# A gated delta rule's recurrence laid out by batch, head and half of the value

## What is computed

```
q = silu(conv4(x Wq) + qcb); k = silu(conv4(x Wk) + kcb) / 8; v = silu(conv4(x Wv) + vcb)
a = sigmoid(x Wa + ba); beta = sigmoid(x Wb + bb)
for each token t:                       # S: 64 values x 64 keys, one for each batch and head
    err = S k_t - v_t
    S   = a_t * S - beta_t * err k_t^T  # a_t scales the rows (values) of S
    o_t = S q_t
o = layernorm over a head's 64 values of o, times ln_w, plus ln_b; o = o * sigmoid(x Wg); x = x + o Wo
```

## Time and profile before

| | us |
|---|---|
| median of three runs | 4137.81 (4136.82 to 4139.02) |
| profiled execution | 4136.74 |
| its span | 4134.7 |
| its setup and start, to the first turning of P | 117.2 |
| recurrence, from there to the last segment's end | to about 2570 |
| the other phases | the rest |

### The profile page before, as it was taken

The page is one execution under the profiler, slowest core; times in us unless marked ns, Lnnn a source line. Parts: engine busy times, 40 slices in busy tenths (PEclk is TensorE's granted clock), DMA queues, the critical chain, the costliest instruction groups (busy, mean ns, idle before and its releaser), DMA issues. The chain is left out here.

```text
span 4134.7 us, 113160 instructions
## 1 busy us (share of the span) xinstructions
PE 3272.3 (79%) x45929; PEld 2781.3 (67%) x45929; DVE 3376.5 (82%) x6184; ACT 2222.6 (54%) x5291; POOL 2340.3 (57%) x3045
## 2 busy tenths in 40 slices
PE   5777787777777777777777774378999979998998
PEld 4677777777777777777777774354666657755765
DVE  4899999999999999999999997216888868856884
ACT  4444444444444454444444442225888779937982
POOL 0667767767767767767767675332000058807860
PEclk9888888898898898888888896588999989998999
DMA  2110110111111111101101100410000011101110
GB/s 75 38 37 26 40 37 27 42 35 28 44 32 33 42 30 36 41 27 38 35 25 36 35 24 24 146 44 1 2 2 2 2 34 37 42 6 38 40 36 26
DMA packets 158097, 139.18 MB, mean 34 GB/s; under 512 B 67204, under 2 KB 110416, under 8 KB 157322
## 3 DMA queue, kind: packets, MB, share of 16 engines
q1 hardware_dynamic: 155274, 129.24, 11.3%
q0 software_dynamic: 2304, 2.71, 0.2%
HBM read 96.11 MB, written 16.82 MB: 27 GB/s over the span
## 5 line engine op out<-in xcount | busy, mean ns | idle before, releaser
L1102 DVE TENSOR_TENSOR a_tmp<-a_h,banks 128x128 f32<-128x128 f32 (+14 forms) x960 | 723.3, 753 | 82.4 <-POOL a_h L871 51.4
L1108 DVE TENSOR_REDUCE a_h<-a_tmp 128x64 f32<-128x128 f32 (+14 forms) x960 | 723.0, 753 | 26.4
L871 POOL TENSOR_TENSOR a_h<-a_h,a_a 128x128 f32<-128x128 f32 (+11 forms) x768 | 552.1, 719 | 174.0 <-DVE a_h L1108 162.8
L540 PE MATMUL banks<-a_xseg,a_w_k 128*128 128x128 f32 x2048 | 308.4, 325 | 138.3 <-DVE a_h L1108 134.4
L540 PEld LDWEIGHTS banks<-a_xseg,a_w_k 128*128 128x128 f32 x2048 | 302.4, 239 | 144.5 <-DVE a_h L1108 140.3
L540 PE MATMUL banks<-a_xseg,a_w_v 128*128 128x128 f32 x2048 | 299.2, 318 | 98.6 <-DVE a_h L1108 98.3
L540 PEld LDWEIGHTS banks<-a_xseg,a_w_v 128*128 128x128 f32 x2048 | 292.9, 233 | 103.8 <-DVE a_h L1108 103.3
L856 POOL TENSOR_TENSOR a_st<-a_st,a_ab 128x512 f32<-128x512 f32 x256 | 326.1, 1274 | 0.0
L613 PE MATMUL banks<-a_wm,a_kt 64*64 64x64 f32 x8192 | 257.2, 221 | 84.6 <-ACT a_wm L746 84.5
L613 PEld LDWEIGHTS banks<-a_wm,a_kt 64*64 64x64 f32 x8192 | 248.4, 137 | 95.8 <-ACT a_wm L746 94.1
L746 ACT ACTIVATE a_wm<-a_wt,k_ih_mask 128x256 f32<-128x256 f32 x512 | 211.4, 495 | 164.1 <-DVE a_wt L1122 164.1
(11 more groups left out here) (297 smaller groups left out, 8422.7 us busy)
## 6 DMA issues: line engine op xcount, KB each, us to landing
a_ab<-decays SPq DMA_DIRECT2D x512, 128.0 KB, 3.0
d_Vs<-d_V SPq DMA_DIRECT2D x128, 128.0 KB, 2.3
sent<-k_nothing SPq DMA_DIRECT2D x40, 64.5 KB, 2.3
b_xe<-sent SPq DMA_DIRECT2D x8, 322.5 KB, 3.2
a_xseg<-xn SPq DMA_DIRECT2D x32, 70.0 KB, 3.1
xn<-a_xnT SPq DMA_DIRECT2D x8, 256.0 KB, 2.8
decays<-a_dc SPq DMA_DIRECT2D x128, 8.0 KB
a_xrow<-in_L_attn_x SPq DMA_DIRECT2D x128, 16.0 KB
```

What stands on the lines that cost most here:

```text
L540: t = e.matmul(b[:, m * SW:(m + 1) * SW].rearrange("p (b t) -> p b t", b=NB), self.wT[n][:, j, ct * P:(ct + 1) * P], xs[:, :, off:off + SE ...
L871: e.tensor_tensor(self.history(ch, t + 1)[:, :, 0:t], self.history(ch, t)[:, :, 0:t], at, ALU.mult).then_inc(*self.s_hist.at((g, t)))
L1102: e.tensor_tensor(prod, both, gram, ALU.mult).then_inc(*step.at((g, t, "product")))
L1108: e.tensor_reduce(self.results(ch, t), prod, AX.X, ALU.add).then_inc(*step.at((g, t, "w")))
```

## The change

All of the recurrence gets another order of partitions: batch (4) x `par` (2) x head pair (8) x half of the values (2), instead of head pair and batch first. So a batch has 32 neighbouring partitions.

- U: the stationary matrix is K by time (32 rows of one batch), the moving one Wt as VectorE turned it; 32 rows hold the two halves' 16 tokens each, and the two halves of the values are neighbouring columns. No masked copy is made, `act_mask` goes. K is no longer doubled (`act_double` goes), its 1/8 moves into Kt's eviction, the Gram evictions and `beta8`.
- P: the stationary matrix is k and q of 16 tokens, interleaved (32 columns of one batch), the moving one the state; the result has tokens on the partitions. Both U and P do two batches in turn, two `par` each, and signal or wait per pair of batches.
- Values and gates (`pe_project_rows`): the stationary matrix is a batch's 32 tokens, the moving one 512 columns of weights, and the result has time on the partitions. The bias is a matmul of one row ahead of the others. One eviction takes 512 columns.
- Gram matrices: tokens of one batch on 32 partitions, two groups instead of four, each with buffers of its own (`Ga`, `Gb`) that one addition of GpSimd joins. Time rows of K: 32 matmuls of full depth instead of 64.
- The stepwise tiles that were by time and then value (a2, bv, P2, o2) are now by value and then time.
- Outputs: after VectorE has turned a segment, TensorE transposes it (`pe_turn`), and ScalarE scales it as it evicts (`act_affine`, 8 instructions of 128x128); the gating works on 128x512 blocks that lie as the projection of g leaves them.
- Setup makes beta by batch on the partitions at once; the transposes and copies go. The decays go to memory in one DMA instead of four.

```diff
-            self.kq = two("kq", [P, R, 3, SEG])
-            self.kraw, self.va = sb("kraw", [P, R, SEG]), sb("va", [P, SEG, R])
-            self.a2, self.bv, self.dc = two("a2_", [P, SEG, 32]), sb("bv", [P, SEG, 32]), two("dc", [P, SEG, 32])
+
+            self.kq = two("kq", [P, R, SEG, 2])
+
+            self.va = sb("va", [P, 32, 32])
+            self.a2, self.bv, self.dc = two("a2_", [P, 32, SEG]), sb("bv", [P, 32, SEG]), two("dc", [P, SEG, 32])
             self.dk = sb("dk", [P, CK, 32])
-            self.G1, self.G1b, self.g2 = sb("g1", [P, 2, CK, R]), sb("g1b", [P, 2, CK, 8]), sb("g2", [P, 2, CK, SEG])
-            self.Kt, self.ST = sb("kt", [P, R, DK]), sb("st", [P, R, DK])
-            self.Wt, self.Wm = sb("wt", [P, R, 32]), sb("wm", [P, R, 2, 32])
+            self.Ga, self.Gb = sb("ga", [P, 2, CK, H0]), sb("gb", [P, 2, CK, H0])
+            self.G1, self.g2 = sb("g1", [P, 2, CK, 32]), sb("g2", [P, 2, CK, SEG])
+
+            self.Kt, self.ST = sb("kt", [P, CH]), sb("st", [P, R, DK])
+            self.Wt = sb("wt", [P, 32, 32])
...
+    def pe_project_rows(self, e, q, n, s, half):
+
+        b = self.take(q, (n, s, half))
+        xs, part = self.xseg[s % 4], slice(half * BANK, half * BANK + BANK)
+        taps = TAPS if n in CONV else 1
+        e.matmul(b, self.c.ones_row[0:1, 0:P], self.bias_row[n][:, part], start=True, stop=False)
+        q.wait_ge(self.l_seg[s % 4], s)
+        for j in range(taps):
+            off = j if taps > 1 else PAD
+            for bi in range(NB):
+                t = e.matmul(b[bi * SEG:(bi + 1) * SEG, :], xs[:, bi, off:off + SEG], self.wT[n][:, j, part], start=False,
+                             stop=(j == taps - 1))
+        t.then_inc(*self.s_full.at((n, s, half)))
+
...
+    def pe_gram(self, e, q, s, par):
+        b = self.take(q, ("gram", s, par))
+        kq, ps = self.kq[s % 2], slice(par * DK, (par + 1) * DK)
+        q.wait_ge(self.s_evac, ("k", s, 1))
+        q.wait_ge(self.s_evac, ("q", s, 1))
+        for ct in range(NCT):
+            for bi in range(NB):
+                r = ct * NB + bi
+                t = e.matmul(b[bi * SEG:(bi + 1) * SEG, ct * 2 * SEG:(ct + 1) * 2 * SEG], kq[ps, r, :, 0],
+                             kq[ps, r].rearrange("p t z -> p (t z)"), start=True, stop=True)
+        t.then_inc(*self.s_full.at(("gram", s, par)))
...
+    def pe_turn(self, e, q, s, half):
+
+        b = self.take(q, ("turn", s, half))
+        q.wait_ge(self.s_turn, s)
+        for m in range(4):
+            i = 4 * (4 * half + m)
+            t = e.transpose(b[:, m * P:(m + 1) * P], self.o1[:, i:i + 4, :].rearrange("p i x -> p (i x)"), self.c.ident[:])
+        t.then_inc(*self.s_full.at(("turn", s, half)))
...
+        for pair in range(0, NB, 2):
             if g:
-                q.wait_ge(self.s_st, (g - 1, r // 8))
-            for par in range(2):
-                ps = slice(par * DK, (par + 1) * DK)
-                t = e.matmul(pb[ps, r * 2 * CK:(r + 1) * 2 * CK].rearrange("p (z t) -> p z t", z=2), self.ST[ps, r, :],
-                             kq[ps, r, 0:3:2, js], start=True, stop=True)
+                q.wait_ge(self.s_st, (g - 1, pair + 1))
+            for ct in range(NCT):
+                for bi in (pair, pair + 1):
+                    for par in range(2):
+                        ps, at = slice(par * DK, (par + 1) * DK), par * BANK + ct * DK
+                        t = e.matmul(pb[bi * SEG:(bi + 1) * SEG, at:at + DK], kq[ps, ct * NB + bi, js].rearrange("p t z -> p (t z)"),
+                                     self.ST[ps, bi * NCT + ct, :], start=True, stop=True)
         t.then_inc(*self.s_p.at(g))
...
-        q.wait_ge(self.s_evac, ("rows", s, 3))
-        for n in range(4):
-            q.wait_ge(self.s_wm, (g, n))
-            if n >= 2:
+        q.wait_ge(self.s_evac, ("rows", s, 1))
+        q.wait_ge(self.s_wt, g)
+        for pair in range(0, NB, 2):
+            if pair:
                 q.wait_ge(self.s_step, (g, "last", "q"))
             elif g:
-                q.wait_ge(self.s_st, (g - 1, n))
-            for m in range(8):
-                r = 8 * n + m
-                for par in range(2):
-                    ps = slice(par * DK, (par + 1) * DK)
-                    t = e.matmul(self.ubank(n)[ps, m * DK:(m + 1) * DK], self.Kt[ps, r, :],
-                                 self.Wm[ps, r].rearrange("p h i -> p (h i)"), start=True, stop=True)
-            t.then_inc(*self.s_u.at((g, n)))
+                q.wait_ge(self.s_st, (g - 1, 1))
+            for ct in range(NCT):
+                for bi in (pair, pair + 1):
+                    rows = slice(bi * SEG, (bi + 1) * SEG)
+                    for par in range(2):
+                        k0, x = ct * P + par * DK, 16 * par + 2 * ct
+                        t = e.matmul(self.ubank(bi)[par * DK:(par + 1) * DK, ct * DK:(ct + 1) * DK], self.Kt[rows, k0:k0 + DK],
+                                     self.Wt[rows, x:x + 2, :].rearrange("p h i -> p (h i)"), start=True, stop=True)
+            t.then_inc(*self.s_u.at((g, pair + 1)))
...
+    def act_project_rows(self, e, q, n, s, half):
+        q.wait_ge(self.s_full, (n, s, half))
+        if n == "v":
+            q.wait_ge(self.s_a2, s)
         elif s:
-            q.wait_ge(self.s_gadd, (s - 1, 3))
-        e.activation(oth, v[:, :, :, 0, :], ACT.Copy, scale=half_of[:, 0:1])
+            q.wait_ge(self.s_vt, s - 1)
+        e.activation(self.va[:, :, 16 * half:16 * half + 16].rearrange("p i x -> p x i"),
+                     self.held((n, s, half)).rearrange("p (x i) -> p x i", i=32),
+                     ACT.Sigmoid if n == "a" else ACT.Silu).then_inc(*self.s_evac.at((n, s, half)))
+
...
-    def act_mask(self, e, q, g):
-
-        q.wait_ge(self.s_wt, g)
-        for n in range(4):
-            rr = slice(8 * n, 8 * n + 8)
-            if g:
-                q.wait_ge(self.s_u, (g - 1, n))
-            for h in range(2):
-                t = e.activation(self.Wm[:, rr, h, :], self.Wt[:, rr, :], ACT.Copy, scale=self.cst["ih_mask"][:, h:h + 1])
-            t.then_inc(*self.s_wm.at((g, n)))
...
+    def act_affine(self, e, q, s, half):
+        key = ("turn", s, half)
+        q.wait_ge(self.s_full, key)
+        if s:
+            q.wait_ge(self.s_y, (s - 1, half))
+        for m in range(4):
+            ct = 4 * half + m
+            t = e.activation(self.oT[:, ct, :], self.held(key)[:, m * P:(m + 1) * P], ACT.Identity, scale=self.lnw[:, ct:ct + 1],
+                             bias=self.lnb[:, ct:ct + 1])
+        t.then_inc(*self.s_evac.at(key))
...
-            at = self.a2[s % 2][:, ch * CK + t, :].rearrange("p (i o) -> p i o", o=1).broadcast_to([P, 32, t])
+            at = self.a2[s % 2][:, :, ch * CK + t:ch * CK + t + 1].broadcast_to([P, 32, t])
...
-        e.tensor_reduce(self.tot[:], self.o2[s % 2][:], AX.X, ALU.add).then_inc(*self.s_tot.at(("mean", s)))
+        e.tensor_reduce(self.tot[:], self.o2[s % 2][:].rearrange("p i t -> p t i"), AX.X, ALU.add).then_inc(*self.s_tot.at(("mean", s)))
     def dve_spread(self, e, q, s):
         q.wait_ge(self.s_squared, s)
         q.wait_ge(self.s_full, ("mean", s))
-        e.tensor_reduce(self.tot[:], self.o1[:].rearrange("p (t x) i -> p t (x i)", x=1), AX.X,
-                        ALU.add).then_inc(*self.s_tot.at(("dev", s)))
+        e.tensor_reduce(self.tot[:], self.o1[:].rearrange("p i t -> p t i"), AX.X, ALU.add).then_inc(*self.s_tot.at(("dev", s)))
...
-        e.tensor_tensor(o2[:, c0:row, :], self.P2[:, 1], self.O.rearrange("p i t -> p t i"), ALU.subtract).then_inc(*self.s_o.at(g))
+        e.tensor_tensor(o2[:, :, c0:row], self.P2[:, :, :, 1], self.O, ALU.subtract).then_inc(*self.s_o.at(g))
         for n in range(4):
             sv = self.ST[:, 8 * n:8 * n + 8, :].rearrange("p r i -> p (r i)")
-            q.wait_ge(self.s_u, (g, n))
+            q.wait_ge(self.s_u, (g, n // 2 * 2 + 1))
...
```

345 lines of the change are left out of this document (153 added, 192 removed).

## The result

The changed kernel takes 4148.0 us (median of 12 runs, 4143.9 to 4152.9), the kernel before 4138.0 (12 runs): ratio 1.0024, interval 1.0015 to 1.0033. It is slower by 10 us; the forecast was 4115 (4095 to 4129). The profiled execution took 4146.99 us.

What follows compares the result with a forecast made beforehand. VectorE, almost without gaps, was taken to set each segment, with the change acting at two seams. (-0.6 + 0.1) x 31 = -16 us, less 6 once only, is -22: forecast 4115 us (4095 to 4129; wider range 4060 to 4200).

Steps and rivals of the forecast that it cites:

- The steps between the seams: 15 recurrence steps between one half's end and the next; instructions left alone, no change priced, no wait of L1102 for L871.
- U and P: TensorE's state updates and P at each seam, 64 matmuls each: 27 ns a record, 3.5 us each.
- the second rival: Same as the large gain: four tiles of 64 columns twice as fast, U 1.9 us; 4038 us, chance 0.17.
- Seam A: Passage between the two halves inside a segment, end of L1122 to L1077: 8.70 us, forecast 0.6 us shorter.
- What VectorE pays: At the seams: reductions L1050, L1055 from 1.18 to 2.0 us; output difference L1131 from 1.23 to 0.7 us.
- The values by time: TensorE's values' projection right before U of seam B: 10.6 us against 8.94, lower end 10.2, upper 15.
- Seam B: Passage between two segments, 10.13 us: P turned 1.8 us later, stall of 1.72 us gone, step 7 +0.1 us.
- Once only: Work outside the segments: -2.9 and some -8 us before the first step, +2.5 us for each of two tails; sum -6.
- The late values: Rival: values' projection ends at 1336.9 and delays U, seam B +4.2 us; 4243 us, halfway 4181; chance 0.25.
- the large gain: Rival: four tiles at 15 ns a record, reductions 1.2 us; seam A -1.6, seam B -1.4; 4038 us, chance 0.17.
- GpSimd comes late: Rival: strided reads slow the running product of the gates (L942) by half, seam B +1.2 us; 4150 us, chance 0.07.
- It cancels: Rival: reductions 2.2 us, U and P unchanged, values 10.6; seam A 0, seam B +0.5; 4146 us, chance 0.13.

Runs made afterwards that it cites:

- run 15: Not a run label: in the quoted words "Between the seams run 15 steps", run is a verb and 15 counts recurrence steps; no kernel, no time.
- e3: Changed kernel with GpSimd's two strided reads of the decays replaced by reads in memory order (wrong values, same sizes and waits): 4113.4 us.
- e2: Changed kernel with the loops of U and P ordered one batch after another, two tiles in turn instead of four: 4233.6 us.
- e1: Changed kernel with TensorE's wait ahead of the values' projection set to the sixth step of the second half instead of the twelfth: 4138.5 us.
- e13: Changed kernel with values' projection at the sixth step, GpSimd's long items (gates included) spread among the histories, beta's decays stored gate first: 4096.6 us.
- e8: Kernel before the change with its values' projection at the sixth step of the second half: 4172.6 us.
- e6: Changed kernel with all decays stored gate first, time last, and the last ones also written to a small tile for the DMA: 4149.0 us.

## Why the prediction was wrong

**The steps between the seams.** This is the step that failed. "Between the seams run 15 steps whose instructions (L1102, L1108) the change leaves alone", the rest of a segment "keep count and size on GpSimd", and "no wait of L1102 for L871" was left. Their instructions kept their size; what they wait for did not: VectorE's waits on GpSimd's histories were 51.4 us before, should have gone, and are 69.6.

In the second half VectorE waits 0.48 us at step 4, behind L889 (1.00 to 1.45 us), and 0.41 at step 8, behind L902 (1.27 to 1.88), because values in their new order meet decays still kept by time: +0.85 a segment, 26 us. e3 removed both waits and gave 35 in all. In the first half the same L889 costs 0.46 at step 4, and 0.44 at step 11 stands behind the subtraction of the mean (L928, 1.91 to 2.36 us, its broadcast operand now read along another axis), which e3 left as it was and which stayed there: 28 us. That the 0.44 is L928's is read from the order and the sizes; no run tests it alone. L894, 0.60 to 0.77, reads no decays and kept its 0.77 in e3; it now reads with a step that belongs to the layout itself. I looked for the stride in the running product (L942, 367 to 376 ns: nothing, as forecast), not in the reads beside it. The Trainium skill's rule of half as much again on reads (GPSIMD Engine Reference, "Performance pitfalls for Q7 kernels"), which the page gives for custom kernels, agrees with L889 and L902 (1.45 and 1.49 times) and not with L942; the row of L912 from which I set it aside writes with a step, and a write is not a read.

**U and P.** "I take 27 ns: 3.5 us each" was the largest mis-sized term of the seams: U took 2.00, close to the end of 1.9 that I gave to the second rival (P, which waits for the adds, 3.04 at seam A). 27 ns is what two tiles in turn measure (e2). The Trainium skill's floor of about 25 ns from start to start (TensorE: Matmul & The Clock Gate, "Wait — 56ns, not 53.3ns?"), which I weighed, does not hold for four tiles: 15.6 ns. Seam A therefore gained 1.6 and not 0.6; VectorE bounds it now, by its adds, a turning and the reduction.

**What VectorE pays.** Reductions 1.85 (2.0 forecast), L1134 0.69 to 0.79 (0.7): right.

**The values by time.** 13.0 us at the place shown and 12.3 in the mean, not 10.6. The second half of the projection took 1.12 and 3.64, so 114 ns a record, four nearly abreast, as priced; the first took 2.07 and 6.36 at the lower level of the clock. The 0.1 us for a change of tile shape, for which the prediction had no row, came out at 0.1 to 0.2: 1.05 us from the bias to the next start where two records at 0.43 are 0.86, and 3.57 from there to U where 3.44 was priced. Before, the lower level lasted from 1318.6 to 1325.4 behind 3.53 us of idle time; now TensorE stands idle for 7.24, because the grams are done sooner, and it lasts to 1330.9. I added the old price of the clock to a new pause.

**Seam B and its stall.** The seam, up to the turning of P, was forecast 1.8 us longer and is 1.84 longer, by two errors that cancel, which is luck: U starts 3.05 us after the end of the turning of W in the mean (3.7 at the place shown), where the prediction had 1.5, and from U's start to the turning of P it is 8.9 us where it had 10.4, since U is 1.5 shorter. "So the stall is gone" failed in part: 1.72 us at step 7 in all of 30 segments became 0.8 us in 16 of them, 0.42 in the mean. With the 0.46 and 0.44 above, the first half fell by 0.48 and not by 1.7. The place shown, with 1.15 us, is one of the worst. The sigmoid was done 6.95 us in the mean behind the start of the turning of P (6.2 to 7.9; 7.8 at the place shown, at 1352.95) and not 5.5: there the evictions of the time rows and of the transposes wait for TensorE twice before they begin. e1 shows the same stall from the other side: what the seam gives up, it takes.

**Once only.** -11.0 at the head (-10.9 forecast), +1.0 behind it (+5). Two slips change nothing: 4136.7 less 22 is 4114.7 and not 4114.5, and the transposes of a segment's outputs are 8 and not 16 (L576, 1.6 to 2.0 us).

**The rivals.** The late values came in kind, at about a third of their price (U 1.5 us later than forecast, 4.1 in that rival), and by the clock and not by the tiles, which ran nearly four abreast; of the large gain the 15 ns a record came true and the reductions at 1.2 us did not; "GpSimd comes late", with the least chance, was the mechanism closest to the truth, by other instructions than I named. That its 4150, and the 4146 of "It cancels", lie so near 4148 is luck: L942 did not slow, and seam A did not stay. Against the forecast for 31 segments seam A brought 32 us more, the first half's steps cost 38 (of which the stall that stayed is 13) and the second half's 26; with 1 us at seam B and 4 less of what comes once, that is 29 of the 33 us by which the forecast missed.

## What to carry over

When a tile's layout is turned, list every reader of it on every engine, and price each by whether both of its operands still run along their rows; an instruction of unchanged size is not an unchanged instruction. Where two chains end within a few us of each other at a seam (here the values' projection on TensorE, and sigmoid, gating and history on GpSimd), taking 2 us from one gives nothing until the other is moved too, and a long item in a saturated queue belongs where the steps' slack is larger than it. The same early projection helped one layout and hurt the other: moving work away from a seam can take the clock with it. And look at more than one place: the segment shown here has a stall of 1.15 us at step 7, and 14 of 30 have none above 0.1 us.

## What the runs showed of the hardware

- Four tiles of TensorE in turn, 64 columns each: 15.6 ns a record (U, 2.00 us for 128); two in turn 27 ns (e2).
- At the granted clock of 0.5 the U of four tiles takes 3.35 us (18 of 29 places at seam B in e13 wholly, 10 for the greater part at that level), that of two up to 6.58 (e8), against 2.00 and 3.95.
- GpSimd reading one operand with a step of 128 bytes: 1.00 to 1.45 us for 384 elements and 1.27 to 1.88 for 512; its instructions of 64 elements hardly change (367 to 376 ns), and with the write of the product turned as well they take 434 (e6).
- VectorE reducing with that step: 1.85 against 1.18 us for 1024 elements.
- A matmul of one row for the bias is not cheaper for its one row: 1.12 us for two records of 512 columns at the full clock and 2.07 at half, where four records of 512 columns with 128 rows took 1.88 at the full clock.
